# One exponential instruction for two neighbouring score tiles in a two-layer cross-attention kernel

## The reference

```python
q = (hidden_states @ Wq).reshape(B, Sq, HEADS, head_dim).transpose(0, 2, 1, 3)
k = (encoder_hidden_states @ Wk).reshape(B, Skv, HEADS, head_dim).transpose(0, 2, 1, 3)
v = (encoder_hidden_states @ Wv).reshape(B, Skv, HEADS, head_dim).transpose(0, 2, 1, 3)
scores = jnp.einsum('bhqd,bhkd->bhqk', q, k) / jnp.sqrt(jnp.asarray(head_dim, q.dtype))
probs = jax.nn.softmax(scores, axis=-1)
...
out = jnp.einsum('bhqk,bhkd->bhqd', probs, v)
out = out.transpose(0, 2, 1, 3).reshape(B, Sq, H)
out = out @ Wo + bo
return out + residual
```

## Time and profile before

| what | value |
|---|---|
| median of 3 runs | 329.85 us (329.51 to 330.17) |
| the profiled execution, its own time | 330.0 us |
| its span, first to last instruction | 328.3 us |
| busy PE, DVE, ACT | 317.6, 255.4, 234.9 us |
| granted TensorE clock | 0.999 of full speed (2.4 GHz) |
| exponentials of the second layer, first and last start | 111.0 and 318.3 us |

### The profile page before, as it was taken

One profiled execution on the slowest core, in us unless ns is written; L12 is line 12 of the kernel. 1 busy time (PEld: TensorE's weight loads), 2 busy tenths in 40 slices (PEclk: granted clock), 3 DMA queues, 4 the chain that ended last, 5 costly groups with the idle time before them and its releaser, 6 DMA issues.

```text
span 328.3 us, 5914 instructions
## 1 busy us (share of the span) xinstructions
PE 317.6 (97%) x1990; PEld 165.5 (50%) x1990; DVE 255.4 (78%) x451; ACT 234.9 (72%) x488; POOL 77.9 (24%) x111
## 2 busy tenths in 40 slices
PE   8999999999999999999999999999999999999995
PEld 7577778856666634434333343343333444434334
DVE  1559587669877889999999999999999889892123
ACT  3537454633445897979978988789798977788982
POOL 5076147370425310010100100101041434102000
PEclk9999999999999999999999999999999999999999
DMA  7960015869995403707218063080540000000002
GB/s 217 314 201 0 2 56 143 244 177 170 159 259 174 164 2 96 101 4 109 38 34 114 0 100 50 17 131 0 89 59 2 2 20 26 20 0 24 1 2 81
DMA packets 15189, 27.92 MB, mean 85 GB/s; under 512 B 2839, under 2 KB 6967, under 8 KB 15159
## 3 DMA queue, kind: packets, MB, share of 16 engines
q1 hardware_dynamic: 14071, 26.41, 36.7%
q10 hardware_dynamic: 1088, 1.14, 1.2%
HBM read 18.19 MB, written 9.18 MB: 83 GB/s over the span
## 4 chain that ended last, share of the span: by engine, by line
PE 82%; DVE 9%; DMA 2%; ACT 2%; issue 2%; SPq 1%; POOL 1%; ACTq 0%; POOLq 0%
PE ps L1372 21%; PE ps L1349 15%; PE ps L1169 14%; PE ps L1360 13%; PE ps L989 9%; DVE mx L870 8%; DMA cs<-in_ctx_dram 2%; PE ps L1121 2%; PE ps L1206 1%; PE ps L1163 1%; ACT probs L658 1%; PE ps L1139 1%; PE ps L1154 1%; SPq L281 1%; SPq L282 1%
## 5 line engine op out<-in xcount | busy, mean ns | idle before, releaser
L870 DVE TENSOR_REDUCE mx<-ps 128x1 f32<-128x512 f32 x320 | 198.7, 683 | 20.6 <-PE ps L1349 19.9
L658 ACT ACTIVATE probs<-ps 128x512 f32<-128x512 f32 x320 | 166.0, 608 | 27.8 <-PE ps L1360 26.0
L1372 PE MATMUL ps<-probs,VS 128*32 128x512 f32 (+1 forms) x680 | 86.3, 579 | 0.3 <-ACT probs L658 0.3
L1349 PE MATMUL ps<-KS,QS 48*128 48x512 f32 x256 | 84.4, 445 | 1.6 <-DVE mx L870 0.7
L1360 PE MATMUL ps<-QS,KS 50*128 50x512 f32 x256 | 79.1, 435 | 0.1
L1349 PEld LDWEIGHTS ps<-KS,QS 48*128 48x128 f32 x256 | 38.3, 184 | 36.3 <-DVE mx L870 27.2
L1360 PEld LDWEIGHTS ps<-QS,KS 50*128 50x128 f32 x256 | 38.4, 185 | 35.9 <-ACT probs L658 28.0
L535 POOL TENSOR_TENSOR attn<-o_turned,o_rec 128x256 f32<-128x256 f32 x9 | 5.6, 621 | 96.2 <-DVE o_rec L884 96.1
L1372 PEld LDWEIGHTS ps<-probs,VS 128*32 128x32 f32 x680 | 13.4, 108 | 25.2 <-ACT probs L658 15.9
L1349 PE MATMUL ps<-KS_last,QS_last 48*128 48x512 f32 x64 | 22.9, 444 | 0.8 <-DVE mx L870 0.7
L640 ACT CAST parts<-ps 128x512 fp32r<-128x512 f32 (+1 forms) x18 | 10.5, 584 | 17.5 <-PE ps L1169 17.1
(11 more groups left out here) (188 smaller groups left out, 412.1 us busy)
## 6 DMA issues: line engine op xcount, KB each, us to landing
KS<-k_parts SPq DMA_DIRECT2D x48, 128.0 KB, 4.3
k_parts<-parts SPq DMA_DIRECT2D x8, 512.0 KB, 3.2
QS<-q_parts SPq DMA_DIRECT2D x48, 64.0 KB, 5.1
q_parts<-parts SPq DMA_DIRECT2D x4, 512.0 KB, 3.5
cs<-in_ctx_dram SPq DMA_DIRECT2D x2, 768.0 KB, 9.8
KS_last<-k_parts SPq DMA_DIRECT2D x12, 128.0 KB, 4.5
xs<-in_x_dram SPq DMA_DIRECT2D x2, 640.0 KB, 6.6
out_dram<-xs SPq DMA_DIRECT2D x7, 160.0 KB, 1.8
```

The lines of the kernel that those rows point to most:

```text
L658: act.activation(probs[:, t % 2 * GH + h, :], ps[:, bank_of["s", m], :], ACT.Exp, scale=float(D1) ** -0.5).then_inc(exp_done, 1)
L870: dve.tensor_reduce(mx[:, g % BUF, at:at + 1], ps[:, bank_of["m", n], :], AX.X, ALU.max).then_inc(max_done, 1)
L1349: pe.matmul(ps[:, bank, :], QS[g % BUF][rows, pair, qt * P:(qt + 1) * P], KS[g % BUF][rows, pair, half * 512:half * 512 + 512], start=True ...
L1372: m = pe.matmul(ps[2 * D1 * h:2 * D1 * (h + 1), bank_of["pv", g], cols], VS[:, g % 2, kt, h, :], probs[:, t % 2 * GH + h, cols], start=(kt ...
```

## The change

A set `two_scores` is computed after the banks have been placed. It holds a score m if m is the first of its step (in the last steps, from 70 on, the first or the third), if its bank and that of score m+1 are neighbours, and if the heads of the step come in the order 0, 1, 2, 3. For these, one exponential instruction covers both banks: it waits until both scores are there, writes both `probs` tiles and raises `exp_done` by two at its end. The second score's own instruction falls away. Nothing else is changed: PE, DVE, POOL and SP have the same instructions in the same order, and the same waits.

```diff
+    two_scores = {m for m in range(GH * STEPS) if (m % 4 == 0 or m % 2 == 0 and m // GH - 1 > LAST_M) and m // GH > 0 and bank_of["s", m + 1] == bank_of["s", m] + 1 and heads(m // GH) == (0, 1, 2, 3)}
...
-                act.wait_ge(s_mm, m + 1)
-                if t >= 2:
-                    act.wait_ge(pv_mm, t - 1)
-                act.activation(probs[:, t % 2 * GH + h, :], ps[:, bank_of["s", m], :], ACT.Exp, scale=float(D1) ** -0.5).then_inc(exp_done, 1)
+                if m - 1 not in two_scores:
+                    w = 2 if m in two_scores else 1
+                    slot, bank = t % 2 * GH + h, bank_of["s", m]
+                    act.wait_ge(s_mm, m + w)
+                    if t >= 2:
+                        act.wait_ge(pv_mm, t - 1)
+                    act.activation(probs[:, slot:slot + w, :], ps[:, bank:bank + w, :], ACT.Exp, scale=float(D1) ** -0.5).then_inc(exp_done, w)
```

## The result

The changed kernel took 333.03 us (median of 4 runs, 332.62 to 335.52) beside 330.01 us of the kernel before (4 runs): ratio 1.0085, 95% interval 1.005 to 1.0121. In a second set of runs it was 333.50 us (6 runs) beside 330.12 us (29 runs), ratio 1.0096, interval 1.0068 to 1.0124. By these ratios it is slower by 2.8 to 3.2 us; the medians themselves differ by 3.0 and 3.4 us. The forecast was 332.0 us, with 330.8 to 333.3 as its range: the first median lies in the upper part of that range, the second just above it.

A forecast was written before the change was run, and what follows sets the result against it. The prediction took PE's queue to bound the kernel. A loss of 2.34 us in eight steps less a gain of 0.22 at the end made 2.1 us on 329.85: 332.0 us, range 330.8 to 333.3.

The forecast's parts named there:

- What bounds the kernel: Whole kernel: PE's queue sets the pace, busy 97% of the span; time it loses is lost for all three engines.
- The double exponential's length: On ACT: one double exponential lasts 1.04 us and saves 0.055 us against two single ones in a back-to-back row.
- The start: Before step 70: the double exponential starts 0.77 us after its step's first score, instead of 0.54 to 0.62.
- the eight steps: Steps 9, 22, 33, 42, 46, 54, 61, 65: fourth score needs the first's bank and starts 0.28 to 0.48 us late.
- What of the delay reaches the value product: Behind the late fourth scores: waits before tile 4 absorb part; value products come 0.12 to 0.48 us later, together 2.34 us.
- The ordinary steps: 17 of 25 double exponentials before step 70: delays up to 0.18 us fit into 0.30 us of room, cost nothing.
- worse: Rival: ordinary steps lose too, 0.07 us in each of six, from a lag of 0.26; 333.7 us, 15 in 100.
- The last steps: From step 70: double exponentials bring steps 74 and 79 forward by 0.11 us each, a gain of 0.22 us.
- A double exponential waits for nothing extra: From step 70: a pair's scores start together, four products in about 0.73 us, so the double one has no added wait.
- The delay is hidden: Rival: PE has slack behind the held steps, so only the gain stays; 329.6 us, 12 in 100.
- Faster: Rival: the 0.055 us saving counts at all 45 places, 2.5 us in total; 327.4 us, 7 in 100.
- Sum: Whole kernel: 2.34 us lost less 0.22 gained gives 2.1 us more, 332.0 us.

The follow-up runs named there:

- e5: Kernel before, all exponentials single; in steps 9, 22, 33, 42, 46, 54, 61, 65 the first waits for both scores: 330.12 us beside 330.12, ratio 0.9991.
- e2: Kernel before with double exponentials only in steps 9, 22, 33, 42, 46, 54, 61 and 65: 332.25 us beside 330.15, ratio 1.0065.
- e9: Kernel before with double exponentials only in steps 9, 20, 22, 33, 42, 46, 54, 61 and 65: 333.20 us beside 329.85, ratio 1.01.
- e1: Changed kernel with single exponentials in steps 9, 22, 33, 42, 46, 54, 61, 65; the other 37 doubles stay: 331.02 us beside 330.15, ratio 1.0029.
- e4: Kernel before with second and third exponential merged in 23 steps up to 67, none in the last steps: 329.93 us beside 330.15, ratio 0.999.
- e7: Kernel before with only the eighteen double exponentials of steps 71 to 79: 330.04 us beside 330.12, ratio 0.9992.
- e10: Kernel before with second and third exponential merged in 23 steps up to 67, plus the double exponentials of steps 71 to 79: 330.22 us beside 329.85, ratio 1.0004.

## Why the prediction was right, point by point

**What bounds the kernel.** Right. The whole loss passed through PE's queue, and nothing gave it back: between the jumps the drift stays level within 0.06 us for up to ten steps.

**The double exponential's length.** 1.04 us forecast, 1.029 measured; two of them in 1.94 us start 0.92 apart (298.74 and 299.66), 0.91 forecast. The rule that the prediction cites from the Trainium skill, "ScalarE: Activation LUTs", section "What ACT_TABLE_LOAD costs", gives 1.04 for the length too; its overlap of 93 ns would have them 0.95 apart, where the rows have 0.92.

**The start.** 0.77 us after score (t,0) forecast, 0.81 in step 8. The sum left out that the trace has the double exponential's wait as an instruction of its own, which ends 0.77 us after score (9,0); the exponential starts 0.045 us behind it. In e5 the single exponential that waits for the same two scores carries its wait itself and starts at 0.77. The distance from score (t,0) to score (t,3) is 1.88 to 1.90 in six of the eight steps (1.85 forecast), in place of 1.37 to 1.49; in step 65 it is 1.93, in step 22 it is 2.16.

**What of the delay reaches the value product.** The sum was right, partly by errors that cancel. The forecast took 0.74 us as the shortest distance from score (t,3) to the value product; in step 8 it is 0.66 (134.46 - 133.80), so 0.04 of later scores and 0.08 of shorter distance gave 0.24 instead of 0.28. Step 22's fourth score cost 0.09 with the eight alone (0.12 forecast) and 0.30 in the full change: there the double exponential starts 1.08 us after score (22,0), and PE waits 0.54 us instead of 0.32. No score is late in it: the instruction that holds the wait ends 0.76 us after score (22,0), as in the other steps, and the exponential starts 0.32 us behind it, in both profiles of the changed kernel, where it is 0.045 in the other seven and in all eight of e2. So the 0.2 us arise on ACT itself, in a time for which the trace shows no wait. They need another of the double exponentials besides the eight; e9 shows that step 20's is not enough, and neither which one it is nor what holds ACT there is known. That 0.30 beside 0.12 hardly shows in the sum of the eight is luck: steps 8, 32, 41, 45 and 53 came out 0.04 to 0.05 below their forecasts.

**The ordinary steps.** Put at nothing, measured 0.3 us (e1 up to step 66: 0.28). The term was 17 times nothing; of its steps 14, 18, 20, 39, 44 and 52 cost 0.04 to 0.07 each. The lateness was forecast rightly, the room was not. The prediction counted its 0.30 us to the start of score (t+1,3) on PE, but what waits for exponential (t,3) is the weight load in front of that score. In step 14 before (exponential (14,3), weight load of score (15,3), value product of step 14):

```profile
147.72 0.62 ACT L658 ACTIVATE probs<-ps 128x512 f32<-128x512 f32 x1
...
148.40 0.19 PEld L1360 LDWEIGHTS ps<-QS,KS 50*128 50x128 f32 x1
...
148.94 0.64 PE L1372 MATMUL ps<-probs,VS 128*32 128x512 f32 x4
```

and in the second profile of the changed kernel (weight load, score (15,3), value product; score (14,0) starts at 145.73 there, at 145.71 before):

```profile
148.59 0.18 PEld L1365 LDWEIGHTS ps<-QS,KS 50*128 50x128 f32 x1 [0.21 <-ACT probs L663]
148.66 0.44 PE L1365 MATMUL ps<-QS,KS 50*128 50x512 f32 x1
...
149.03 0.64 PE L1377 MATMUL ps<-probs,VS 128*32 128x512 f32 x4
```

Before, the weight load started 0.06 us after the exponential's end (148.34), so there was no room to speak of. Now the exponential ends 0.18 us later, as forecast, and the weight load waits for it. Score (15,3) starts only 0.02 us later but lasts 0.44 us instead of 0.39, and the value product comes 0.07 us later. Steps 18, 39, 44 and 52 show the same pattern. The view of waits agrees: in e1 five more weight loads of scores waited for exponentials than before, in e4 none more (first the kernel before, then e1).

```profile
PEld ps L1360 <- ACT probs L658: 34.9, 50, 0.8
PEld ps L1365 <- ACT probs L663: 35.9, 55, 0.8
```

Step 20 is of another kind. It is one of five steps (5, 6, 15, 20, 30) that do their value product in two halves, the first of them in front of `pair(2)`; the description of PE's queue above leaves that out. The first half needs exponential (20,3), which now ends 2.81 us after score (20,0), and it starts at 2.86 where it started at 2.81. So this is the mechanism of the rival "worse", at a lag of 0.18 us where the prediction let it begin at 0.26.

**The last steps.** This step failed: a gain of 0.22 us was forecast, and they cost 0.13 (0.08 + 0.14 - 0.05 - 0.04). Two things were wrong. "A double exponential waits for nothing extra" isn't so. In e7 the one of step 72 starts at 300.98, 0.62 us after the first score of its pair (300.36), where a single one starts 0.54 after the earlier trace rows; about half of these 0.08 us is again the wait that stands in front as an instruction of its own. The saving was somewhat larger than the 0.11 forecast: in step 79 four single exponentials took 2.07 us from the first one's start to the last one's end, two double ones in e7 1.94. Of these 0.13 us 0.05 was left at each of the two places. And the transfer of the maxima was not in the sum at all: the double one in step 70 waits for a second score that a reduction on DVE holds back, the copy behind it in ACT's queue is late, and with it the scores of the last group. e7 takes that one double exponential out, and the 0.23 us are gone.

**The rivals.** "The delay is hidden" is out by e2, and with it the reading in the prediction by which a share of weight loads of 50% leaves PE slack: in the second profile that share is still 50%, and each late product shifted the end. "Faster" is out by e4 and e10: 23 and 41 double exponentials for whose late releases nothing waits save 0.01 and 0.19 us by drift, and nothing that the time can tell.

**Sum.** Forecast 2.1 us: 2.34 for the eight, -0.22 for the end. Measured by drift 2.8 us: 2.36 + 0.31 + 0.13. The median moved by 3.0 us, with an interval from 1.6 to 4.0. The mechanism of the eight steps was right and makes most of the loss; the missing 0.7 us are the two terms put at nothing and at a gain.

## What to carry to other kernels

Merging two instructions makes the first one's result, and the buffer it frees, as late as the second's. Before counting the saved start, list for each buffer who takes it next and how much later that comes than the release: here PE waited 0.3 to 0.5 us at 8 of 45 places, and these made three quarters of the loss by themselves. Count the room up to the weight load that stands in front of a matmul, not up to the matmul: here it was 0.06 us and not 0.30. Of the instructions queued behind the merged one, look also at the small copies that start a transfer; one of them had only 0.1 us to spare.

## What the runs showed of the hardware

The pace of one execution repeats to a few hundredths of a microsecond: seven of the eight jumps agree within 0.02 us between the changed kernel's first profile, its second and e2. What differs between executions is almost all before the second layer: the first score of step 0 came between 0.98 us earlier and 1.12 us later than in the profile before, in eleven other traces. In front of step 70 the double exponentials whose wait ended last started 0.045 us after the instruction with their wait, at every place but one (0.32 us in step 22, in both profiles of the changed kernel). And one execution ran for a few microseconds near 114 us at the lower clock (0.74 granted on average over 6 us), and its drift rose by 1.5 us between steps 0 and 1; the same kernel's second profile has neither.
